# Attention block of 8 images: the rows of mean, scale and bias move behind the second chunk of scores, the denominators behind the third group of weighings

## The reference

```python
x: (8, 32, 32, 64)
xn = group_norm(x, gamma, beta)          # mean and variance of each group of 8 channels of an image
xf = xn.reshape(B, N, C)                 # N = 1024, C = 64
q = xf @ wq + bq; k = xf @ wk + bk; v = xf @ wv + bv
attn = softmax(einsum('bnc,bmc->bnm', q, k) * C ** -0.5)
out = einsum('bnm,bmc->bnc', attn, v) @ wp + bp
return xf + out
```

## Time and profile before

| | |
|---|---|
| median of 3 runs | 193.49 us (193.38 to 201.9) |
| the profiled execution | 193.45 us |
| its span, first to last instruction | 191.6 us |
| PE busy / DVE / ACT / POOL | 184.7 / 134.3 / 112.5 / 142.2 us |
| granted TensorE clock | 1.00 throughout |

### The profile page before, as it was taken

The page is one execution under the profiler, slowest core; times in us unless marked ns, Lnnn a source line. Parts: engine busy times, 40 slices in busy tenths (PEclk is TensorE's granted clock), DMA queues, the critical chain, the costliest instruction groups (busy, mean ns, idle before and its releaser), DMA issues.

```text
span 191.6 us, 3318 instructions
## 1 busy us (share of the span) xinstructions
PE 184.7 (96%) x1234; PEld 96.5 (50%) x1234; DVE 134.3 (70%) x179; ACT 112.5 (59%) x184; POOL 142.2 (74%) x92
## 2 busy tenths in 40 slices
PE   7989899999999999999999999999999999999992
PEld 7655455344643755355643655355542745444442
DVE  3589766875797856878586856867587847719753
ACT  3594687669645665569645665468545655258611
POOL 4167595999999899995999599995999499950000
PEclk9999999999999999999999999999999999999999
DMA  6596000000000000001000010001000000001002
GB/s 142 201 393 225 0 0 0 5 2 2 0 0 3 26 33 3 0 2 58 0 0 0 20 41 0 0 2 58 0 0 5 26 31 0 0 5 55 3 23 87
DMA packets 4415, 6.95 MB, mean 36 GB/s; under 512 B 832, under 2 KB 1456, under 8 KB 4400
## 3 DMA queue, kind: packets, MB, share of 16 engines
q1 hardware_dynamic: 4400, 6.75, 10.2%
HBM read 4.59 MB, written 2.10 MB: 35 GB/s over the span
## 4 chain that ended last, share of the span: by engine, by line
PE 87%; DMA 5%; DVE 3%; SPq 2%; issue 1%; ACT 0%; DVEq 0%
PE attn L868 29%; PE scores L810 26%; PE wide L781 12%; DMA values<-in_x_dram 3%; PE misc L892 3%; PE scores L765 3%; PE scores L771 3%; PE misc L876 2%; DMA max_rows<-max_T 2%; PE misc L752 2%; PE misc L883 1%; DVE chunk_max L602 1%; PE misc L796 1%; PE misc L898 1%; DVE y_out L730 1%
## 5 line engine op out<-in xcount | busy, mean ns | idle before, releaser
L315 POOL TENSOR_TENSOR prob_sum<-prob_sum,probs 128x1024 f32<-128x1024 f32 x42 | 100.7, 2397 | 5.9
L602 DVE TENSOR_REDUCE chunk_max<-wide 128x1 f32<-128x1024 f32 x60 | 73.4, 1223 | 31.2 <-PE wide L781 30.6
L416 ACT ACTIVATE probs<-scores 128x1024 f32<-128x1024 f32 x64 | 63.3, 1022 | 30.1 <-PE scores L810 29.0
L868 PE MATMUL attn<-probs,values 128*64 128x512 f32 x256 | 62.0, 605 | 0.0
L781 PE MATMUL wide<-k_hi,q_hi 64*128 64x512 f32 x120 | 30.7, 472 | 1.3 <-DVE chunk_max L602 1.0
L868 PEld LDWEIGHTS attn<-probs,values 128*64 128x64 f32 x256 | 15.5, 136 | 26.5 <-issue 24.1
L315 POOL TENSOR_TENSOR prob_sum<-probs 128x1024 f32<-128x1024 f32 x7 | 16.7, 2379 | 11.3 <-ACT probs L416 11.3
L781 PEld LDWEIGHTS wide<-k_hi,q_hi 64*128 64x128 f32 x120 | 12.5, 183 | 22.1 <-DVE chunk_max L602 12.1
L810 PE MATMUL scores<-q_hi,step_hi 64*128 64x512 f32 x96 | 20.8, 426 | 0.4
L810 PE MATMUL scores<-q_lo,step_hi 64*128 64x512 f32 x96 | 19.2, 391 | 0.0
L810 PE MATMUL scores<-q_hi,step_lo 64*128 64x512 f32 x96 | 19.2, 390 | 0.0
(11 more groups left out here) (144 smaller groups left out, 236.2 us busy)
## 6 DMA issues: line engine op xcount, KB each, us to landing
x_T<-in_x_turned_dram SPq DMA_DIRECT2D x8, 256.0 KB, 6.7
values<-in_x_dram SPq DMA_DIRECT2D x8, 256.0 KB, 6.8
out_dram<-y_out SPq DMA_DIRECT2D x7, 256.0 KB, 2.0
out_dram<-y_out SPq DMA_DIRECT2D x2, 128.0 KB, 1.7
max_rows<-max_T SPq DMA_DIRECT2D x14, 4.0 KB
packed<-in_packed_dram SPq DMA_DIRECT2D x1, 192.0 KB, 3.8
packed<-in_packed_dram SPq DMA_DIRECT2D x1, 130.5 KB, 2.5
bp_all<-in_bp_dram SPq DMA_DIRECT2D x1, 32.0 KB, 4.5
```

The lines of the kernel that those rows point to most:

```text
L315: nc.gpsimd.tensor_tensor(prob_sum[b % 2][:, :], so_far[:, :], probs[i][:, :], ALU.add).then_inc(sum_done, 1)
L416: nc.scalar.activation(probs[i][:, :], scores[flip_of(b, i)][:, :], ACT.Exp, scale=SCALE).then_inc(exp_done, 1)
L602: nc.vector.reduce_max(chunk_max[:, p, j:j + 1], made_in[:, :], AX.X).then_inc(max_done, 1)
L868: product = nc.tensor.matmul(attn[x_half * C:(x_half + 1) * C, :], values[b][:, t * C:(t + 1) * C], probs[i][:, x_half * HALF:(x_half + 1) ...
```

## The change

In rounds 1 to 6:
- PE: `rows_of(p)` moves from before chunk 4 to behind chunk 1, ahead of tiles 2 and 3, together with the wait for `y_done`. `group_mean(z)` and `denominators(b - 1)` move from behind weighing group 1 (before chunk 3) to behind weighings 2 and 3 (before chunk 5; in round 6 behind weighing 2) and wait there for `residual_done`. `turn_denominators` moves from behind chunk 4 to behind chunk 6.
- DVE: `centre(p)` moves from behind the reduction of chunk 4 to behind that of chunk 1, `scale` from behind chunk 5 to behind chunk 2 and `normalise`, `add_bias` from behind chunk 6 to behind chunk 3, `invert` (line 613) from behind chunk 4 to behind chunk 6. Round 1 has one `scale` and one `add_bias` more, of image 0, and they move along.
- ACT: the copies of mean and denominators move from ahead of exponential 4 to ahead of exponential 6, behind `scale_w_vp`; `sum_squares(z)` from ahead of exponential 5 to ahead of exponential 7.

Round 0 and round 7 stay as they are. The diff (left out: round 6 on PE, written out by itself, with the same moves):

```diff
--- before.py
+++ after.py
@@ -500,14 +500,12 @@
                     round_step(1)
                     copy_mean(2)
                     sum_squares(2)
-                if exists(z):
                     copy_mean(z)
                 if b == LAST:
                     scale_w_vp(b - 1)
-                if b > 0:
                     copy_den(b - 1, misc)
                 exp_tile(b, 4)
-                if exists(z):
+                if b == 0:
                     sum_squares(z)
                 exp_tile(b, 5)
                 if b == 0:
@@ -519,7 +517,12 @@
                     gain_of(s)
                 if 0 < b < LAST:
                     scale_w_vp(b - 1)
+                    if exists(z):
+                        copy_mean(z)
+                    copy_den(b - 1, misc)
                 exp_tile(b, 6)
+                if b > 0 and exists(z):
+                    sum_squares(z)
                 if b == 0:
                     act.wait_ge(centred_T_done, 2)
                     act.wait_ge(gain_done, 2)
@@ -564,8 +567,6 @@
                     dve.wait_ge(first_mean_row_made, 1)
                 else:
                     dve.wait_ge(rows_made, s)
-                    if s >= 2:
-                        dve.wait_ge(den_turned, s - 1)
                 nc.vector.tensor_tensor(pixels(values[s][:, :]), pixels(values[s][:, :]), per_channel(misc[:, MEAN_ROW]),
                                         ALU.add).then_inc(centred_done, 1)
 
@@ -685,24 +686,32 @@
                 if b >= 2:
                     finish(b - 2)
                 reduce_chunk(p, 1, wide)
+                if b > 0:
+                    centre(p)
                 reduce_chunk(p, 2, wide)
                 if b > 0 and exists(s):
                     normalise(s)
+                if b == 1:
+                    scale(0)
+                if b > 0:
+                    scale(p)
                 reduce_chunk(p, 3, wide)
+                if b == 1:
+                    add_bias(0)
+                if b > 0:
+                    add_bias(p)
                 reduce_chunk(p, 4, wide)
                 if b == 0:
                     add_eps(2, misc[:, 0:1])
-                if b > 0:
+                    centre(p)
+                reduce_chunk(p, 5, wide)
+                if b == 0:
+                    scale(p)
+                reduce_chunk(p, 6, wide)
+                if b == 0:
+                    add_bias(p)
+                else:
                     invert(b - 1, misc)
-                centre(p)
-                if b == 1:
-                    scale(0)
-                reduce_chunk(p, 5, wide)
-                if b == 1:
-                    add_bias(0)
-                scale(p)
-                reduce_chunk(p, 6, wide)
-                add_bias(p)
                 reduce_chunk(p, 7, wide)
                 if exists(z):
                     add_eps(z, misc[:, 2 * P:2 * P + 1])
@@ -987,6 +996,14 @@
                         start_tile(b, i)
                         subtract_max(b, i)
                 next_max_chunk(p, 1)
+                if b == 1:
+                    pe.wait_ge(var_eps_done, 4)
+                    pe.wait_ge(maxT_copied, 1)
+                elif b > 1:
+                    pe.wait_ge(y_done, b - 1)
+                if b > 0:
+                    pe.wait_ge(gain_done, p)
+                    rows_of(p)
                 next_tile(b, 2)
                 next_tile(b, 3)
                 next_max_chunk(p, 2)
@@ -994,43 +1011,37 @@
                 weigh_values(b, 1)
                 if b == 0:
                     pe.wait_ge(q_lo_done, 2)
-                elif b == 1:
-                    pe.wait_ge(var_eps_done, 4)
-                    pe.wait_ge(maxT_copied, 1)
-                else:
-                    pe.wait_ge(y_done, b - 1)
-                if b == 0:
                     pe.wait_ge(sum_T_done, 2)
                     group_mean(2, misc[:, 2 * P + 1:2 * P + 2])
-                if exists(z):
-                    pe.wait_ge(sum_T_done, z)
-                    group_mean(z, misc[:, 2 * P:2 * P + 1])
-                if b > 0:
-                    pe.wait_ge(sum_done, SUMS * b)
-                    denominators(b - 1, prob_sum[(b - 1) % 2], misc)
+                    pe.wait_ge(sum_T_done, 3)
+                    group_mean(3, misc[:, 2 * P:2 * P + 1])
                 next_max_chunk(p, 3)
                 next_tile(b, 4)
                 next_tile(b, 5)
-                if exists(z):
-                    pe.wait_ge(mean_done, z - 1)
                 if b == 0:
+                    pe.wait_ge(mean_done, 2)
                     pe.wait_ge(bias_out_done, 1)
-                else:
-                    pe.wait_ge(den_copied, b)
-                pe.wait_ge(gain_done, p)
-                rows_of(p)
+                    pe.wait_ge(gain_done, 1)
+                    rows_of(1)
                 next_max_chunk(p, 4)
                 if b == 0:
                     pe.wait_ge(squares_done, 3)
                     group_variance(2, misc[:, 0:1])
-                if b > 0:
-                    turn_denominators(b - 1, misc)
                 weigh_values(b, 2)
                 weigh_values(b, 3)
+                if b > 0:
+                    pe.wait_ge(residual_done, residuals_up_to(p))
+                    if exists(z):
+                        pe.wait_ge(sum_T_done, z)
+                        group_mean(z, misc[:, 2 * P:2 * P + 1])
+                    pe.wait_ge(sum_done, SUMS * b)
+                    denominators(b - 1, prob_sum[(b - 1) % 2], misc)
                 next_max_chunk(p, 5)
                 next_tile(b, 6)
                 next_tile(b, 7)
                 next_max_chunk(p, 6)
+                if b > 0:
+                    turn_denominators(b - 1, misc)
                 weigh_values(b, 4)
                 weigh_values(b, 5)
                 next_max_chunk(p, 7)
...
```

## The result

The changed kernel took 203.35 us, the median of 4 runs (203.28 to 206.14), against 194.16 us for the kernel before (4 runs of the same measurement, 193.38 to 201.9). The ratio of the means, 204.03 to 193.90 us (without the run of 201.9), is 1.0523, 95% interval 1.04 to 1.0645. The profiled execution took 203.39 us with a span of 201.6 us, 10.0 us more than before.

A forecast was written before the change was run, and what follows sets the result against it. PE bounds the kernel, busy 184.7 of 191.6 us. Round 1's 1.30, four rounds at 1.72 and round 6's -0.1 sum to 8.1 us over 193.45; with the median at 193.49 it said 201.6 us, range 198.0 to 203.8.

The forecast's parts named there:

- 0.29 for the release: DVE's `normalise`, held by POOL's running addition, ends 0.29 us behind it; a whole run behind it would mean 0.65.
- The rows save next to nothing: PE's moved rows: 0.47 us saved against 0.30 to 0.51 paid, so +0.17 to -0.04 us a round gained.
- the large term is DVE: `normalise` on DVE, issued too late, delays the reduction of chunk 3 and PE's chunk 4: 1.72 us a round, four times.
- the catch in rounds 2 to 5: DVE's `normalise` is issued 0.15 to 0.36 us too late and waits for the end of POOL's second addition.
- the first rival: DVE's `normalise` is not caught in rounds 2 to 5: 194.4 us, same speed; chance 0.12.
- 193: Time in us if `normalise` is not caught in rounds 2 to 5 and round 1 too is free.
- Half the rounds caught: Only half of the rounds have `normalise` held by POOL's addition: 198.0 us; chance 0.05.
- rows vanished: PE's rows vanish wholly in the wait for exponentials, 0.47 us back in each of five rounds: 191.1 us; chance 0.02.
- the next gap lost too: `normalise` also waits for POOL's third addition, 2.53 us more in each of four rounds: 211.7 us; chance 0.03.
- The sign named for it: Line 561, `normalise` on DVE, at about 2.4 to 2.6 us in rounds 2 to 5 if the forecast holds.
- The first rival's mark: PE's tile 2 starting by 88.0 in round 3, so rows of 0.45 us or less, would leave `normalise` uncaught.
- at full clock: PE's granted clock, read as full in the kernel before; the sum has no term for a fall.

The follow-up runs named there:

- e7_noadd: Changed kernel with POOL's second addition of rounds 1 to 5 cut to one column instead of 1024: 194.57 to 195.0 us at a clock of 1.0, ratio 1.002.
- e2_later: Changed kernel with `normalise` moved from behind the reduction of chunk 2 to behind that of chunk 4: 193.59 to 193.62 us at a clock of 1.0.
- e1_form: Changed kernel with `normalise` in a form that also writes a sum to an unused column: 194.24 to 194.69 us at a clock of 1.0.
- e8_both: Changed kernel with `normalise` behind the reduction of chunk 4 and round 1's `scale(0)` ahead of that of chunk 2: 193.54 to 193.93 us at a clock of 1.0.
- e3_warm: Changed kernel with five zero-weight matmuls in PE's wait ahead of chunk 4: 201.4 and 201.65 us at a clock of 1.0, 202.79 at 0.987.
- e6_nudge640: Kernel before, with a memset of 640 columns on DVE ahead of `normalise`: 193.74 and 193.81 us at 0.996 or 0.997, ratio 1.003.
- e9_nudge_reduce: Kernel before, with a maximum over x_T on DVE ahead of `normalise`: 195.43 and 195.78 us at clocks of 0.999 and 0.997, ratio 1.0103.

## Why the prediction came out as it did

**Confirmed, step by step.** Times of round 3 from the trace of the changed kernel, less the 3.33:

| step | forecast | measured |
|---|---|---|
| rows start | 87.55 | 87.54 |
| tile 2 | 88.14 to 88.35 | 87.93 and 88.23, by halves |
| group 1 | 89.85 to 90.06 | 90.00 |
| `normalise` issued | 91.11 to 91.32 | 91.26 |
| POOL's second addition starts | 90.96 | 90.98 |
| `normalise` ends | 93.63 | 93.65 |
| chunk 4 | 95.42 | 95.44 |
| group 2, chunk 6 | 95.85, 100.17 | 95.86, 100.18 |
| group 3 | 100.97 | 100.97 |
| rounds 2 to 4, each | +1.72 | +1.74, +1.73, +1.72 |
| round 1; round 6 on | +1.30; -0.1 | +1.26; -0.13 |

In round 1 chunk 4 started at 52.15 - 0.33 = 51.82 and group 3 at 57.36, both as forecast to a hundredth. The choice of 0.29 for the release, against a whole run behind the addition, held: 0.29 in round 3. The Trainium skill, SBUF — State Buffer, section "A bandwidth-pool intuition that's wrong (but worth ruling out)", has a blocked transfer's descriptors go on some 115 ns after DVE's end; carried over to DVE and with a whole run behind it, that gives an estimate of 0.65, and the measurement decides for 0.29. The exclusive lock of the section "Who interferes with whom" is borne out by `e7_noadd`, 0.54 us against 2.39.

**"The rows save next to nothing" and "the large term is DVE".** Shown by `e2_later` and `e7_noadd`: without the catch in rounds 2 to 5 the change takes 193.6 to 195.0 us at full clock, where the kernel before takes 193.3 to 194.0. `e7_noadd` is the first rival made real: 194.57 to 195.0 us, where its sum was 194.4. `e1_form`, free in round 1 too, took 194.24 to 194.69 where the prediction said 193. That 193 left out the two `scale` steps of round 1, which cost there even when the step is free: chunk 4 of round 1 still waited 0.69 us in this trace. And the step is 0.26 us longer in every round (0.80 for 0.54).

**The rivals.** Half the rounds caught, rows vanished, the next gap lost too: none occurred; all five instructions of line 561 are at 1656 to 2391 ns. The sign named for it, 2.4 to 2.6 us, was set a little high against the prediction's own times (93.63 less 91.11 to 91.32 is 2.31 to 2.52); the measured 2.35 to 2.39 of rounds 2 to 5 fit these. The first rival's mark, tile 2 by 88.0, was badly chosen: tile 2's first half did start at 87.93, ahead of the rows' last matmul, yet its second half only at 88.23, and the chunk and the group behind it came as late as with a whole tile started at 88.14 to 88.35 (group 1 at 90.00).

**The step that failed** is the clock, "at full clock": a term of the sum that was put at nothing. The prediction read the granted clock of the kernel before, 1.00 throughout, and used it for both sides: its sum starts from 193.45 and has no term for the clock of the changed kernel. The sum came true where that holds: 201.33 to 201.51 us in four later runs at a clock of 1.0, against 193.31 to 193.97 for the kernel before (six of the ten such runs beside the experiments up to 193.44), +8.0 us where +8.1 was forecast. In the first measurement it did not hold: all four runs had a clock of 0.989 to 0.992. The span grew by 8.04 us through the named terms (1.26 + 1.74 + 1.73 + 1.72 + 1.72 - 0.13), by 1.63 through the fall in round 5, and by 0.33 ahead of round 1, where the start varies between runs (the same matmul at 42.81 in one trace of the changed kernel and 42.38 in the other): 10.0. The median was thus 203.35 and not 201.6. That it lies inside the range of 198.0 to 203.8 is luck, for the range was widened for other reasons, and the mean of the four, 204.03, lies above it; the run of 206.14 us does that, and its cause stays open. The kernel before has such a term as well, 194.7 to 195.0 us at 0.988 against 193.4 at 1.00. The missing term was 1.3 to 1.6 us on either side of the comparison, and 3.2 in three later runs of the changed kernel. Whether the new waits make a fall likelier isn't settled: one trace has it right behind such a wait, another has the same wait without it. Beside the experiments 23 of 49 runs of the kernel before were at 0.988 or 0.989; of the 11 of the changed kernel, counting all measurements, 7 were at 0.981 to 0.992. So few runs don't tell the two apart.

## What to carry to other kernels

When an edit moves a large elementwise step of VectorE between SBUF buffers by a few tenths of a microsecond, set its new start against GpSimd's instructions before counting what the edit saves: here 0.45 us later on DVE cost 1.72 us a round, ten times the most that the moved matmuls could save (0.17). Such a step that ends "just in time" at a gap has no margin, and an instruction of that line that lasts four times its median is the sign to look for. And give the sum a term for a clock fall, from the spread of the runs of before, even where the profiled one shows 1.00 throughout: the three runs ahead of this forecast (193.38, 193.49 and 201.9 us) were too few to show it, the fourth (194.82) and those beside the experiments did, at 1.3 to 1.6 us.

## What the runs showed that was not expected

- **A memset of VectorE holds GpSimd up, a reduction doesn't.** Three additions took 7.40 us beside the reduction, 7.75 with a memset of 128 x 256 and `normalise` in their gap, 8.17 with one of 128 x 640 and `normalise`. The kernel before, with `normalise` alone in the gap, is at 7.65.
- **The start shown of a GpSimd addition is not the moment from which it holds the other.** `normalise` was not held 0.11 us behind it, with a memset ahead, and was held 0.28 and 0.45 behind it. Where the limit lies without a memset was not measured.
- **`normalise` has a third duration**: 0.36 us behind a memset, against 0.54 in the kernel before and where the addition was shrunk to a column. Its cause was not tried.
- **The clock fell to 0.50 in a stretch of full work.** One trace of a changed-kernel variant, `e8_both`, in the head: PE was busy for 0.98 us of the us in which the fall begins, and for all of each us at 0.50:

```profile
7.00:8.00 1.00, 0.98 (x6) 0.62 (x7) 0.87 (x6) 0.35 (x2) 0.00 (x0) 0.85 0.51 191
8.00:9.00 1.00, 1.00 (x4) 0.00 (x0) 0.00 (x0) 0.60 (x2) 0.00 (x0) 0.50 0.94 359
9.00:10.00 1.00, 1.00 (x4) 0.51 (x4) 0.54 (x1) 0.00 (x0) 0.32 (x1) 0.50 1.05 406
10.00:11.00 1.00, 1.00 (x4) 0.00 (x0) 0.80 (x2) 0.00 (x0) 0.00 (x0) 0.50 1.06 408
```

  The traces of `e3_warm`, `e6_nudge640`, `e7_noadd` and `e9_nudge_reduce` show it at the same place, at mean clocks of 0.987 to 0.991; why it comes in some executions only is open. The runs of `e8_both` at 0.987 and 0.988 took 195.02 and 195.2 us, against 193.54 to 193.93 at 1.0. The kernel before is 1.3 us longer at such a clock, but none of those runs was profiled.
